# Second mixture of experts: slots are named by products of zeros and ones, and tokens are gathered instead of scattered

## The reference

```python
z = xf @ proj_w.T + proj_b                       # 2048 tokens, 8 experts
s = sigmoid(z) + expert_bias
probs = softmax(log(clip(s, 1e-12)))
topk_w, topk_idx = top_k(probs, 2)               # weights divided by their sum
wmat = where(assigned, pair_w, -inf)             # 8 x 4096
kept_w, kept_pair = top_k(wmat, 640)             # an expert keeps at most 640 pairs
xe = xf[kept_tok]
h = gelu(xe @ fc1_w.T + fc1_b)                   # 512 wide, per expert
oe = h @ fc2_w.T + fc2_b
y = zeros.at[kept_tok].add(oe * kept_w)
sh = gelu(xf @ sh1_w.T + sh1_b) @ sh2_w.T + sh2_b   # shared part, 1024 wide
x = x + tanh(g_ffn[1]) * (sh + y)
```

## Time and profile before

| | |
|---|---|
| median of three runs | 1140.48 us |
| lowest, highest | 1139.31, 1146.55 us |
| the profiled execution's time | 1146.95 us |
| its span, first to last instruction | 1145.2 us |
| PE busy | 985.4 us (86%) |
| DVE, ACT, POOL busy | 774.3, 595.7, 250.8 us |
| mean granted clock of PE | 0.926 of 2.4 GHz |

### The profile page before, as it was taken

How to read it: one execution, slowest core, us unless ns; L and a number is a source line. 1 busy time by engine, 2 the same in 40 slices (tenths; PEclk the granted TensorE clock), 3 DMA queues, 4 the chain that set the end, 5 groups by cost and what they waited for, 6 DMA issues and landing times. The chain is left out here.

```text
span 1145.2 us, 23305 instructions
## 1 busy us (share of the span) xinstructions
PE 985.4 (86%) x8394; PEld 913.4 (80%) x8394; DVE 774.3 (68%) x1978; ACT 595.7 (52%) x1439; POOL 250.8 (22%) x343
## 2 busy tenths in 40 slices
PE   3799998677799577999999999999977997899992
PEld 3688886567688456989999999999977996789992
DVE  5687777677576657878677767766777672356655
ACT  3566665243397425555555555555546442376660
POOL 3443433125000440010101000010000006425542
PEclk9899999857898878999999999999988998799996
DMA  8421111001255220101011010103030002445317
GB/s 260 143 68 39 58 39 38 1 1 56 64 185 131 74 80 1 44 1 44 1 44 44 1 44 1 43 1 117 1 100 13 1 1 98 131 146 178 125 50 253
DMA packets 75212, 77.94 MB, mean 68 GB/s; under 512 B 19680, under 2 KB 66272, under 8 KB 74976
## 3 DMA queue, kind: packets, MB, share of 16 engines
q1 hardware_dynamic: 68992, 62.33, 17.4%
q0 software_dynamic: 4992, 13.90, 3.4%
q10 hardware_dynamic: 1120, 0.27, 0.1%
HBM read 46.53 MB, written 29.95 MB: 67 GB/s over the span
## 5 line engine op out<-in xcount | busy, mean ns | idle before, releaser
L1494 PE MATMUL a_psK<-a_kvThi,a_wk 128*128 128x512 f32 x256 | 97.9, 423 | 3.1 <-DVE a_klo L1679 1.7
L307 POOL TENSOR_SCALAR t_neg<-t_raw,t_nthr 128x256 bf16<-128x256 f32 (+1 forms) x54 | 60.8, 1142 | 109.7 <-DVE t_nthr L498 109.7
L1551 PE MATMUL a_psY<-a_nwhi,a_uhi 128*128 128x256 f32 x256 | 73.8, 288 | 5.1 <-DVE a_ulo L1707 5.1
L1658 POOL TENSOR_TENSOR a_toklo<-a_kv,a_tokhi 128x512 fp32r<-128x512 f32 x16 | 22.1, 1384 | 243.5 <-ACT a_tokhi L1586 243.5
L1601 ACT ACTIVATE a_probs<-a_psS,a_nmax 128x256 f32<-128x256 f32 x128 | 59.6, 471 | 29.3 <-DVE a_nmax L1689 29.3
L1534 PE MATMUL a_psU<-a_pTlo,a_tokhi 128*128 128x256 f32 x256 | 72.4, 283 | 0.0
L1534 PE MATMUL a_psU<-a_pThi,a_tokhi 128*128 128x256 f32 x256 | 72.4, 283 | 0.0
L1534 PE MATMUL a_psU<-a_pThi,a_toklo 128*128 128x256 f32 x256 | 72.4, 283 | 0.0
L1551 PE MATMUL a_psY<-a_nwlo,a_uhi 128*128 128x256 f32 x256 | 72.3, 282 | 0.0
L1551 PE MATMUL a_psY<-a_nwhi,a_ulo 128*128 128x256 f32 x256 | 72.2, 282 | 0.0
L1591 ACT ACTIVATE a_khi<-a_psK,a_bk 128x512 fp32r<-128x512 f32 x64 | 44.1, 688 | 51.3 <-PE a_psK L1494 51.3
(11 more groups left out here) (366 smaller groups left out, 3256.2 us busy)
## 6 DMA issues: line engine op xcount, KB each, us to landing
t_raw<-in_L_ffn_expert_w SPq DMA_DIRECT2D x16, 512.0 KB, 3.8
f_raw<-in_fc_T SPq DMA_DIRECT2D x16, 512.0 KB, 3.8
m_turned<-m_sorted SPq DMA_DIRECT2D x8, 680.0 KB, 5.2
m_sorted<-a_zeros SPq DMA_DIRECT2D x8, 640.0 KB, 3.5
m_results<-a_zeros SPq DMA_DIRECT2D x8, 512.0 KB, 4.5
m_sorted<-m_zeros SPq DMA_DIRECT2D x1, 3072.0 KB, 12.7
e_xin<-m_sorted SPq DMA_DIRECT2D x24, 128.0 KB, 2.6
m_expert_out<-e_y SPq DMA_DIRECT2D x24, 128.0 KB, 1.7
```

The costliest lines, as they stand in the source:

```text
L307: ins = pool.tensor_scalar(neg[:, own], raw[h % NRAW][:, own], nthr[h % 2][:, n:n + 1], None, ALU.is_lt)
L1494: ins = pe.matmul(psK[:].rearrange("p b t -> p (b t)"), wk[x][:, a, h * DH:(h + 1) * DH], kvT[pair % 2][y][:, a, :, :, :].rearrange("p b m ...
L1551: ins = pe.matmul(psY[:, b, :], u[ch % 2][x][:, f, hh * P:(hh + 1) * P], nw[y][:, f, 2 * j + hh, :], start=first, stop=last, skip_group_ch ...
```

## The change

`m1_sorted` with its tags, its clearing and the scatters are gone. The normed rows go to DRAM as they are, `m1_tokens`, 2048 rows of 256, by two DMAs of SP at the start of the stage. For each slot the number of its token has then to be known. It is found in the asides behind place_all. Of each of the 32 sets (two choices by 16 blocks) of 128 pairs, `one_row` holds at [pair, set, r] a one where the pair's slot has row r in its tile, and `one_tile` at [pair, set, t] a one where it lies in tile t of the 40. `named` is one_tile times the pair's partition + 1, and one_tile times the set's number. 32 bf16 products of PE, one_row (128 x 128) by named (128 x 80), summed in PSUM, then give for each slot, in the partition of its row, both numbers; zero is an empty slot. Six small operations make of them `comes`, the row to gather, and `goes`, the row in m1_results.

- Aside slots: tile_up is in slot 2 of pair 4; the first half of one_row and of the products in slot 3 of pair 4; the second half in slot 0 of pair 5; index_all in slot 1 of pair 5.
- POOL gathers the tiles of experts 0 to 2 (15 indirect DMAs), those of expert 2 once expert 0's tiles are turned, and then one tile of expert e+3 behind each send of expert e. `xin` lies in the first ten blocks of the buffer of the normed rows. PE waits for each tile on a semaphore of its own.
- All rounds of the experts have the order TURNS; FIRST and SECOND are gone.
- The bias goes from POOL to DVE, behind every other put. top2 turns four iotas into numbers where it turned one.

```diff
-                TP, RT = CAP // P, 2 * NB // NE
-                sp.wait_ge(s["const_done"], 3)
+                RT = 2 * NB // NE
+                sp.wait_ge(s["const_done"], 1)
                 for e in range(NE):
                     sp.wait_ge(s["k_done"], e * NU // NE + 1)
-                    rows = xg[e * CAP:(e + 1) * CAP]
-                        sp.dma_start(rows[:, D:ROW].rearrange("(t p) d -> p t d", p=P),
-                                     spare[:, e * TP:(e + 1) * TP, :].bitcast(F32)).then_inc(s["zeroed"], 16)
-                    sp.dma_start(rows[:, 0:D].rearrange("(t p) d -> p t d", p=P), zeros[:].unsqueeze(1).to_broadcast([P, TP, D]))\
-                      .then_inc(s["zeroed"], 16)
...
-                pool.memset(m["rows"][:, :, D:], 0.0)
                 pool.memset(zeros[:], 0.0).then_inc(s["const_done"], 1)
-                pool.memset(spare[:], 0).then_inc(s["const_done"], 1)
-                pool.wait_ge(s["const_done"], 2)
-                pool.iota(spare[:, :, 0], pattern=[[P, NE * CAP // P]], base=2 * NB * P, channel_multiplier=1).then_inc(s["const_done"], 1)
...
-            return ("place" if n == ROUNDS else ""), 0
+            return {ROUNDS: "place", ROUNDS + 1: "tile", ROUNDS + 2: "spread", ROUNDS + 3: "spread", ROUNDS + 4: "index"}.get(n, ""), n - ROUNDS - 2
...
+                sp.dma_start(xr_b[:, 0:LAST, :], rows_sb[:, 0:LAST, :]).then_inc(s["rows_out"], 16)
                 load_w1(0)
                 load_w1(1)
                 load_w2(0)
                 load_w2(1)
+                sp.wait_ge(s["row_done"], 2)
+                sp.dma_start(xr_b[:, LAST:NB, :], rows_sb[:, LAST:NB, :]).then_inc(s["rows_out"], 16)
...
-                sp.wait_ge(s["up"], PAIRS * NQ)
-                for h in range(2):
-                    sp.wait_ge(scattered[0][h], NB // 2 * 16)
-                load_x(0)
                 load_w1(2)
-                for h in range(2):
-                    sp.wait_ge(scattered[1][h], NB // 2 * 16)
-                load_x(1)
                 load_w1(3)
                 load_w2(2)
-                load_x(2)
...
+                    elif what == "spread":
+                        pe.wait_ge(s["tiled"], 1)
+                        for half in range(CHUNKS // 2):
+                            chunk_ = r * CHUNKS // 2 + half
+                            pe.wait_ge(s["spread"], chunk_ + 1)
+                            for n in range(chunk_ * SETS // CHUNKS, (chunk_ + 1) * SETS // CHUNKS):
+                                ins = pe.matmul(psW, one_row[:, n, :], named[:, n, :, :], start=(n == 0), stop=(n == SETS - 1))
+                        if r == 1:
+                            ins.then_inc(s["listed"], 1)
...
+                def gather(e, t):
+                    if t == 0:
+                        at_least(pool, s["turned"], (e - 1) * NT)
+                    pool.indirect_dma_start(xin[e % 2][:, t, :], None, xr, bass.IndirectOffsetOnAxis(ap=comes[:, e * NT + t:e * NT + t + 1], axis=0))\
+                        .then_inc(x_in[e % 2][t], 16)
...
+                pool.wait_ge(s["rows_out"], 32)
+                pool.wait_ge(s["n_turned"], NB)
+                pool.wait_ge(s["indexed"], 1)
+                for e in range(3):
+                    for t in range(NT):
+                        gather(e, t)
                 for e in range(NE):
                     for t in range(NT):
                         send(e, t)
-                        if t == 2 and there(e + 2):
-                            read_index(e + 2)
-                        if t % 2 == 0 and done < NB:
-                            bias(done)
-                            done += 1
+                        if there(e + 3):
+                            gather(e + 3, t)
...
-                    k.step(dve.tensor_tensor(lost[:], lost[:], token[:], ALU.mult))
-                    dve.tensor_tensor(into[:], lost[:], at[:], ALU.add).then_inc(s["placed"], 1)
+
+                    k.step(dve.scalar_tensor_tensor(out=slot_i[:], in0=lost[:], scalar=float(NSLOT), in1=at[:], op0=ALU.mult, op1=ALU.add))
+                    dve.tensor_scalar(row_i[:], slot_i[:], P - 1, None, ALU.bitwise_and)
+                    k.step(dve.tensor_scalar(tile_i[:], slot_i[:], 7, None, ALU.logical_shift_right))
+                    dve.tensor_copy(row_b[:], row_i[:].rearrange("p n b -> p (n b)"))
+                    k.step(dve.tensor_copy(tile_b[:], tile_i[:].rearrange("p n b -> p (n b)")))
+
+                def tile_up():
+
+                    k.step(dve.tensor_tensor(one_tile, count_b[:, 0:TILES].unsqueeze(1).to_broadcast([P, SETS, TILES]),
+                                             tile_b[:].unsqueeze(2).to_broadcast([P, SETS, TILES]), ALU.is_equal))
+                    dve.tensor_scalar(named[:, :, 0, :], one_tile, self_f[:, 0:1], None, ALU.mult)
+                    dve.tensor_tensor(named[:, :, 1, :], one_tile, block_b[:].unsqueeze(2).to_broadcast([P, SETS, TILES]), ALU.mult)\
+                       .then_inc(s["tiled"], 1)
                     k.step(dve.tensor_tensor(wk[:], ws[:], has[:], ALU.mult))
-                    k.step(dve.tensor_scalar(wk[:], wk[:], gates[:, 3:4], None, ALU.mult))
+                    dve.tensor_scalar(wk[:], wk[:], gates[:, 3:4], None, ALU.mult)
+
+                def spread(r):
+                    for n in range(r * CHUNKS // 2, (r + 1) * CHUNKS // 2):
+                        own = slice(n * SETS // CHUNKS, (n + 1) * SETS // CHUNKS)
+                        dve.tensor_tensor(one_row[:, own, :], count_b[:].unsqueeze(1).to_broadcast([P, SETS // CHUNKS, P]),
+                                          row_b[:, own].unsqueeze(2).to_broadcast([P, SETS // CHUNKS, P]), ALU.is_equal).then_inc(s["spread"], 1)
+
+                def index_all():
+
+                    dve.wait_ge(s["listed"], 1)
...
                         elif kind == "d" and there(e):
                             put(e, n)
+                            if n % 2 == 0 and e * 3 + n // 2 < NB:
+                                bias(e * 3 + n // 2)
```

More of the change, by code:

```diff
@@ L2163, in _ @@
                 for e in range(-1, NE):
[L2164 removed]
+                    for k, (kind, n) in enumerate(TURNS):
                         if kind == "u" and there(e + 1):
                             xgelu(e + 1, n)
[L2168 removed]
+                        before, last = TURNS[k - 1] if k > 0 else ("", 0)
                         if before == "u" and there(e + 1):
@@ new lines, in spread @@
+                def spread(r):
[5 more added lines that the diff above has]
+                    dve.wait_ge(s["listed"], 1)
+                    k.step(dve.tensor_copy(value[:], psW[:, 0, :]))
+                    k.step(dve.scalar_tensor_tensor(out=value[:], in0=psW[:, 1, :], scalar=float(P), in1=value[:], op0=ALU.mult, op1=ALU.add))
+                    dve.tensor_scalar(from_i[:], value[:], -1.0, 0.0, ALU.add, ALU.max)
+                    k.step(dve.scalar_tensor_tensor(out=none[:], in0=value[:], scalar=0.0, in1=empty[:], op0=ALU.is_equal, op1=ALU.mult))
+                    dve.scalar_tensor_tensor(out=goes[:], in0=value[:], scalar=-1.0, in1=none[:], op0=ALU.add, op1=ALU.add)
+                    dve.tensor_scalar(comes[:], from_i[:], NTOK - 1, None, ALU.bitwise_and).then_inc(s["indexed"], 1)
@@ L2383, in aside @@
                         place_all()
+                    elif what == "tile":
+                        tile_up()
+                    elif what == "spread":
+                        spread(r)
+                    elif what == "index":
+                        index_all()
                 def w1_lo(e):
@@ L2410, in put, with bias @@
                     dve.tensor_tensor(y[n % NY][:], psY[n % 2][:, 0, :], xb2[:, e, :], ALU.add).then_inc(s["y_done"], 1)
+                def bias(i):
+                    dve.wait_ge(s["kept"], i + 1)
+                    dve.tensor_tensor(x_sb[:, i, :], x_sb[:, i, :], b2s[:], ALU.add).then_inc(s["x_biased"], 1)
+                assert 3 * NE >= NB
                 rows_in()
```

138 lines of the change are left out of this document (52 added, 86 removed).

## The result

The changed kernel takes 1149.52 us (median of 9 runs, 1146.06 to 1153.58) against 1139.35 us for the kernel before (9 runs beside it): ratio 1.0087, interval 1.0061 to 1.0113. One of the nine runs of the kernel before, at 1190.44 us, was a slow execution and doesn't enter the ratio. Forecast were 4.6 us less; measured are 10.2 us more. The profiled execution has a span of 1147.8 us in a time of 1149.52.

A forecast was written before the change was run, and what follows sets the result against it. PE, busy 86% of 1145.2 us, was taken to lose 21.7 us beside the scatters and more at the experts' start. Tail -1.3 and experts' start -3.3 gave -4.6 us: median 1135.9 us, range 1127 to 1157.

The forecast's parts named there:

- The two stops: Shared part's tail: PE waits for DVE's flags after down(4), 11.1 us, and up(6,1), 5.5, plus 3.8 of slow clock.
- The index and the start of the gathers: Behind up(6,3): lists ready at 972.3 us, POOL issues ten gathers until 985.8, hidden by down(5) to down(7).
- The rival that POOL becomes the limit: Expert rounds: longer DMA issue makes a round 17.3 instead of 15.35 us, +10 us, 1146 us; chance 0.10.
- The experts' start: First two expert rounds: transposes between matmuls make them 24.9 instead of 28.2 us, -3.3 us.
- if the slow stretch doesn't come: Shared part's tail: condition for ending at 991.8 instead of 993.1 us, -1.3 us; PE's gaps counted at nothing.
- The rival: Slow stretch comes back beside ten back-to-back gathers from 972.3 us: 19.7 us, giving 1155.6 us; chance 0.24.
- All 21.7 us of the loss must be there without the profile too: Shared part's tail: PE's whole loss beside the scatters taken as present unprofiled, since profile and median differ by 6.5 us only.
- the second load of x: Experts' start: a second loss, the load issued only at 997.8 us after the second scatter; first rounds take 28.2 us.

The follow-up runs named there:

- a_late: Changed kernel with PE's 32 products in one place behind up(7,1), the index behind them (late products): 1121.22 us, ratio 0.9841.
- a_order: Changed kernel with the order of before (FIRST, SECOND) at the experts' start: 1153.7 us, ratio 1.0103.
- l_order: The late-products kernel (a_late) with the order of before at the experts' start: 1134.73 us, ratio 0.9935.
- a_straight: Changed kernel with POOL's 40 gathers replaced by straight loads on SP, index made but unused: 1141.91 us, ratio 1.0001.
- a_paced: Changed kernel where POOL pauses after five gathers until PE has done the whole of down(6): 1145.12 us, ratio 1.0014.
- b_quiet: Kernel before without all 32 scatters and the waits for them: 1121.04 us, ratio 0.985.
- b_quiet2: Kernel before without its 32 scatters again, on another chip: 1124.73 us, ratio 0.9843.
- b_same2: Kernel before, unchanged, profiled again: 1140.42 us, ratio 1.0002.
- group 4: Runs on one chip with the kernel before beside them (median 1143.1 us); the unchanged changed kernel took 1148.39 us there, ratio 1.0049.
- group 2: Repeats of both kernels unchanged on one chip (kernel before's median 1142.1 us); the changed kernel took 1149.74 and 1151.63 us.
- a_same2: Changed kernel, unchanged, profiled again: 1151.63 us, ratio 1.0085.
- a_same3: Changed kernel, unchanged, profiled again on another chip: 1148.39 us, ratio 1.0049.
- b_half: Kernel before with only the first 16 of its 32 scatters: 1123.16 us, ratio 0.9869.
- a_late2: The late-products kernel (a_late) a second time, on another chip: 1130.06 us, ratio 0.9892.
- a_late3: The late-products kernel (a_late) a third time: 1131.55 us, ratio 0.9903.
- a_late4: The late-products kernel (a_late) a fourth time, as a control: 1120.28 us, ratio 0.9829.

## Why the prediction was wrong, point by point

Against the profiled execution the steps add up. From the ranks to the end, before took 209.2 us (57.7 + 151.5), so the forecast was 204.6; the changed kernel took 210.4, 5.8 more. The forecast median, 1135.9 us, lies 13.6 below the measured one: these 5.8, then 1.4 before the ranks, where nothing is changed, and 6.5 that the forecast took over as the distance of profile and median; the changed kernel's profiled execution lies at its median.

**The two stops: right.** Predicted 11.1 + 5.5 + 3.8 = 20.4. Measured: up(6) starts at 954.28 instead of 944.2 (where a_late has it, with its ranks at the same time), 10.1 us; up(6,2) at 963.79 instead of 958.6, 5.2; the two groups of 24 take 4.42 and 4.74 us instead of 2.9, 3.4 in all: 18.7 us. The clock fell after both stops, to 0.50, that is 1.2 GHz, as after the idle time of the earlier trace rows. The tensor_tensor over 1280 elements took 1.48 and 1.49 us, as priced; the Trainium skill ("VectorE: DVE Perf Modes", "What auto-detection actually checks") doubles such an operation only if every tensor is 16-bit with step 1 or -1; the trace agrees, since one operand here has step 0 and 1.48 us is the price of one element a cycle. The tensor_scalar took 0.55, not the 0.85 carried over from the earlier trace rows; the 0.5 estimated from the page was nearer.

**The index and the start of the gathers: right.** DVE ends the lists at 971.8 us (predicted 972.3), POOL issues from 972.60 to 985.3 (972.3 to 985.8), and no transpose waits for a gather. The rival that POOL becomes the limit didn't come: gathers and sends fit into a round.

**The experts' start: right, and then spent.** The first two rounds take 25.7 us (from the first up at 1000.40 to 1026.1) instead of 28.2, predicted 24.9. The order is worth 3 to 5 us (a_order, l_order). But from the first transpose to the end the kernel takes 151.6 us, as before, since gaps and longer rounds beside gathers and sends took it back: without gathers on POOL it is 148.2 (a_straight), and there the first two rounds take 24.6 us, close to the forecast.

**"if the slow stretch doesn't come": the first step that failed.** It was put at nothing in the sum, and it came back with the gathers, at a fifth of its former size: 4.0 us in down(6). Behind the first transpose 3.4 us more were lost, where none was expected: 2.4 by the gaps of three rounds, the rest in the first two rounds, without a gap. The row against it, sends that left PE busy 98.30 of 98.30 us, didn't hold here, with a gather behind each send. The rival had named the place (beside the first ten gathers), the cause (DMAs issued back to back; it holds for this place by a_straight and a_paced) and the delay (10 us; it was 9.9). Its price was too high: 19.7 us were taken over from 32 scatters, and a chain of ten ends 12.7 us after it began, so less than 3 us of it are left after a delay of ten. The rows for this were there: the length of the chain and the delay. Instead of a chance of 0.24 for 19.7 us, a term of its own of about 3 us was due. Sum against the forecast: -1.7 for the stops, +4.0 in down(6), +3.4 behind the transpose, together 5.7 of the 5.8 us.

**"All 21.7 us of the loss must be there without the profile too": the second.** They were there in that execution and not in the others. b_quiet and b_quiet2 put the scatters at 17.5 and 18.4 us in the medians, and the two other traces of before take 204.3 and 205.4 us from the ranks to the end instead of 209.2. The reason given, that profile and median differ by 6.5 us only, allowed for just this: the profiled execution was one of the longer ones, and 4 of its 6.5 us lay in this stage. By carrying the whole difference over as a constant, the forecast took 21.7 us off an execution that had lost 17 or so. Where PE's stretch is short, the second load of x and the sends, both behind the scatters, become what PE waits for (b_same2). The prediction listed that load as a loss of its own, next to the stretch; they overlap.

**What is left.** In one sum, from medians where there are some: scatters -18 (b_quiet, b_quiet2), order -4 (a_order, l_order), stops and products +18.6 (traces of a_straight and b_quiet, 54.7 less 36.1), gathers beside PE +8.8 (a_straight): +5.4 us. Measured were +5.3 (group 4), +7.6 and +9.5 (group 2) and +10.2 (at first). The sum meets the lowest of the four. The traces say nearly the same: from the ranks to the end the four of the changed kernel average 211.1 us and the three of before 206.3, 4.8 more. What the other 2 to 5 us of the medians are is open: before the ranks, where nothing is changed, the four traces average 935.0 us and the three 935.5, so it isn't there in the traces.

## What to carry to other kernels

Put a small product that waits for another engine where its input has long been made: the same 32 products cost 18.6 us of stops and slow clock in one place and 1.3 us some slots further on, and the kernel with that one move beats both (1.0 to 1.7% under the kernel before). When an engine is slow beside a chain on another, look whether the chain's end releases it next: then a shorter slow stretch alone may gain little (in b_same2 PE gave 8 us back), and the engine's loss in one trace isn't what the removal of the chain gives. Leave the chain out once and measure; here that gave 17.5 us. And take the loss of an irregular stretch from more than one trace: here it was 21.6, 17.0 and 7.7 us.

## What the runs showed of the hardware

PE runs in bursts with no releaser while POOL issues indirect DMAs back to back. In all eight traces with such gaps before the transposes, scatters or gathers, the first burst behind a gap starts 9.9 to 13 us after the first DMA of a chain of ten or more: 9.9 in each trace with the changed kernel's chain, 10.1, 12.9 and 13.0 in the three of before, with bursts mostly 1.4 us apart, and 0.7 in a_same2, a_same3 and a_order. Before the transposes they were absent with straight loads on SP and with a chain cut in two. But they were absent in b_half too, through 22 us of a chain of 16, and in b_same2 they ended at 964.4 us while the scatters went on to 994.2, so a chain alone is not enough. The kernels with late products hardly test it: their long products end 10.8 to 10.9 us after the first gather in a_late, a_late2, a_late3 and a_late4, where one burst would have been left. The stall of 4.2 us starts there in two of these four; whether it is the same thing is open. What stops PE is open as well. The Trainium skill ("Runtime: NRT & Kernel Launch", "Instruction fetch mechanics") has each engine fetch its instructions in blocks of 16 KiB through a DMA queue. The trace of the changed kernel has such a queue, here from 950 to 1000 us (packets, MB, share):

```profile
q8 instruction: 3, 0.05, 0.5%
```

Its three packets lie at 954.9, 974.2 and 997.2 us, none in or right before the gaps from 982.5 to 986.8, so a block that comes late isn't seen there. In before its packets lie at 943, 971 and 998 us, and the gaps run from 956 to 983, on both sides of the middle one. l_order's stall of 4.2 us has no packet either, a_late2's has one (974.3). This case doesn't show whether it is the cause.
